# Retention plus FP4 feed-forward: in eight steps of the second half, VectorE splits the next x before it takes h's maximum instead of after h's inverse

## The reference

```
def fp4_quant_dequant(x):
    xb = x.reshape(shape[:-1] + (shape[-1] // 16, 16))
    scale = maximum(max(abs(xb), -1) / 6, 1e-12)
    xn = xb / scale
    q = GRID[searchsorted(MID, abs(xn))] * sign(xn) * scale
x1  = layernorm(x + retention(x))                # 8 heads, gate, projection
gate = fp4(x1) @ fp4(w_gate).T                   # 256 -> 704
up   = fp4(x1) @ fp4(w_up).T                     # 256 -> 704
h    = silu(gate) * up
out = layernorm(x1 + fp4(h) @ fp4(w_down).T)     # 704 -> 256
```

## Time and profile before

| | |
|---|---|
| median of 3 runs | 577.37 us |
| profiled execution | 577.54 us |
| its span in the trace | 575.6 us |
| PE busy | 558.3 us, 97% |
| DVE busy | 514.5 us, 89% |
| ACT busy | 363.9 us, 63% |
| POOL busy | 239.5 us, 42% |
| granted PE clock, mean | 0.997 |

### The profile page before, as it was taken

How to read it: one execution, slowest core, us unless ns; L and a number is a source line. 1 busy time by engine, 2 the same in 40 slices (tenths; PEclk the granted TensorE clock), 3 DMA queues, 4 the chain that set the end, 5 groups by cost and what they waited for, 6 DMA issues and landing times.

```text
span 575.6 us, 14088 instructions
## 1 busy us (share of the span) xinstructions
PE 558.3 (97%) x4408; PEld 482.1 (84%) x4408; DVE 514.5 (89%) x1193; ACT 363.9 (63%) x931; POOL 239.5 (42%) x291
## 2 busy tenths in 40 slices
PE   7999999999999999999999999999999999999993
PEld 4788888888888888888888788889999989999983
DVE  7667878999999999899999889999999999999996
ACT  4455766777686676777668654556555766676563
POOL 2211121534435344343534323665665665665430
PEclk9999999999999999999999999999999999999998
DMA  7611110110111011011001000000000110010013
GB/s 210 225 35 32 56 47 12 56 54 1 54 55 34 21 55 46 9 55 55 27 27 36 19 11 10 1 0 2 2 1 2 38 38 2 19 38 20 2 36 109
DMA packets 24984, 22.31 MB, mean 39 GB/s; under 512 B 2026, under 2 KB 21875, under 8 KB 24947
## 3 DMA queue, kind: packets, MB, share of 16 engines
q1 hardware_dynamic: 24130, 20.27, 11.4%
q10 hardware_dynamic: 816, 1.57, 0.8%
HBM read 17.63 MB, written 4.20 MB: 38 GB/s over the span
## 4 chain that ended last, share of the span: by engine, by line
PE 71%; DVE 18%; issue 5%; POOL 2%; DMA 2%; ACT 1%; DVEq 0%; ACTq 0%; POOLq 0%
PE wide_banks L1415 40%; PE wide_banks L1486 9%; PE wide_banks L1631 5%; PE wide_banks L1463 4%; DVE shared L891 3%; PE wide_banks L1474 3%; PE turn L1512 3%; PE turn L1449 2%; DVE h_amax L875 2%; DVE shared L1121 2%; PE wide_banks L1499 2%; PE wide_banks L1603 2%; DVE win_lo L1008 2%; POOL shared L1368 1%; DVE shared L896 1%
## 5 line engine op out<-in xcount | busy, mean ns | idle before, releaser
L1379 POOL TENSOR_TENSOR shared<-shared,h_scale 128x704 f32<-128x704 bf16 x31 | 43.0, 1389 | 81.9 <-DVE shared L896 79.4
L1415 PE MATMUL wide_banks<-win_hi,x_hi 128*128 128x512 f32 x192 | 65.5, 422 | 3.1 <-DVE shared L711 1.5
L1486 PEld LDWEIGHTS wide_banks<-shared 128*128 128x128 f32 x512 | 62.0, 192 | 2.8
L484 ACT ACTIVATE shared<-opened,rstd 128x64 f32<-128x64 f32 x240 | 63.5, 339 | 1.1
L1415 PE MATMUL wide_banks<-wgu_hi,xq_hi 128*128 128x512 f32 (+1 forms) x192 | 60.2, 395 | 1.4 <-DVE xq_lo L1113 1.3
L1486 PE MATMUL wide_banks<-shared 128*128 128x64 f32 x512 | 60.6, 271 | 0.0
L1415 PE MATMUL wide_banks<-win_hi,x_lo 128*128 128x512 f32 x192 | 60.3, 395 | 0.0
L1415 PE MATMUL wide_banks<-win_lo,x_hi 128*128 128x512 f32 x192 | 60.3, 395 | 0.0
L1415 PE MATMUL wide_banks<-wgu_lo,xq_hi 128*128 128x512 f32 (+1 forms) x192 | 56.5, 375 | 0.0
L1415 PE MATMUL wide_banks<-wgu_hi,xq_lo 128*128 128x512 f32 (+1 forms) x192 | 56.4, 375 | 0.0
L450 ACT ACTIVATE shared<-shared 128x704 bf16<-128x704 f32 x32 | 25.3, 789 | 44.9 <-POOL shared L1368 43.4
(11 more groups left out here) (156 smaller groups left out, 1472.3 us busy)
## 6 DMA issues: line engine op xcount, KB each, us to landing
xf<-in_x_feat SPq DMA_DIRECT2D x32, 128.0 KB, 2.2
tab<-in_tables SPq DMA_DIRECT2D x16, 256.0 KB, 2.7
xt<-in_x_tok SPq DMA_DIRECT2D x32, 128.0 KB, 2.1
out<-x SPq DMA_DIRECT2D x32, 128.0 KB, 1.7
x<-in_w_in ACTq DMA_DIRECT2D x3, 512.0 KB, 5.3
w<-in_w_gu SPq DMA_DIRECT2D x1, 1408.0 KB, 7.7
w<-in_w_down SPq DMA_DIRECT2D x1, 704.0 KB, 8.9
wgu_lo<-pow_dram SPq DMA_DIRECT2D x1, 576.0 KB, 4.8
```

What stands on the lines that cost most here:

```text
L484: last = act.activation(gated[:, b, cols], opened[:, b, cols], ACT.Copy, scale=rstd[:, b, 1 + k:2 + k])
L1379: pool.tensor_tensor(over_blocks(hq[:, b]), over_blocks(h_steps[:, b]), spread(h_fp4["scale"][:, b]), ALU.mult).then_inc(h_fp4["ready"], 1)
L1415: last = pe.matmul(dst, lhs, rhs, start=k == 0, stop=k == len(parts) - 1)
L1486: last = pe.matmul(mixed[:, r, DV * at:DV * (at + 1)], ret[:, slot(k)], vs[:, b, DV * k:DV * (k + 1)], start=False, stop=k >= HEADS - 2, s ...
```

## The change

In steps 4 to 11 (`QUAD` is 4, `EIGHT` is 8), DVE's `split_xq(n + 1)` is issued behind `add_out` and in front of `h_max(n - 1)`; in all other steps it stays behind `h_inverse`. The instruction, its operands and its semaphore wait on `xq_hi_ready` are the same. No other engine's code changes.

```diff
@@ ffn_body of DVE
                 if out:
                     add_out(n - 5, 1 - b)
+                ahead = QUAD <= n < EIGHT + QUAD
+                if ahead:
+                    split_xq(n + 1, 1 - b)
                 if quant:
                     dve.wait_ge(h_done, n)
                     h_max(n - 1)
@@
-                if valid(n + 1) and n > 0:
+                if valid(n + 1) and n > 0 and not ahead:
                     split_xq(n + 1, 1 - b)
```

## The result

The changed kernel takes 578.3 us (median of 21 runs, 577.91 to 578.57), the one before 577.37 (21 runs, 577.06 to 577.9). The ratio is 1.0015, 95% interval 1.0008 to 1.0021: slower by 0.9 us (0.5 to 1.2). I had forecast 577.2, slightly faster. The profiled execution took 578.27 us with a span of 576.2 at a granted clock of 0.997, as before.

A forecast was written before the change was run, and what follows sets the result against it. DVE's chain of waits, which releases PE at step 19, was taken to bound the kernel. Changes over steps 4 to 11 summed to -0.16 us, taken as -0.2 from the median 577.37: 577.2 us, range 576.5 to 578.3.

The forecast's parts named there:

- What bounds it: DVE's chain of waits up to PE's step 19 sets the end; PE could win back at most 2.36 us.
- Part 1: PE gets `xq_lo` about 2 us earlier, but its second part then waits for the product, so PE alone keeps no gain.
- Part 2: DVE's ordinary step, counted from `add_out`'s start: `split_h` to the product 0.21 us earlier, h's inverse 0.07 us later.
- Part 3: Which shift reaches L891: steps 6, 7 -0.21 each, 10, 11 +0.07 each, 5 0, 4 -0.07, 9 -0.09, 8 +0.28 us.
- PE keeps what it wins: Rival: PE's stalls in steps 4 to 18 are its own, up to 2.36 us back, 575.0 us; chance 0.07 of over 1.15.
- The early split waits: Rival: L1113 waits for `xq_hi` beyond step 8, or longer there; sum +0.3 to +1.0 us, 577.6 to 578.4; chance 0.12.
- The scale misses its turn: Rival: POOL's L1362 gets in before DVE's scale, reciprocal 0.59 us later; 3.1 us in all, 580.5; chance 0.13 for over 1.15.
- step 32: Evidence against the missed turn: the scale started 0.04 us ahead of L1379's recorded end and still took only 0.17 us.

The follow-up runs named there:

- the two failed mends: Changed kernel with the chain operation of steps 5 to 7 ahead of `add_out`: 579.07 us; likewise with picked split steps, early in 6, 7, 13, 14, 15: 578.64 us.

## Why the prediction was wrong

**What bounds it: right.** PE's gain of 0.74 us in step 5 was real and went to the product at once. The end moved with DVE's chain: +0.87 us from rounding to rounding over steps 4 to 18, +0.93 between the medians.

**Part 1, PE: right.** Step 5's first matmul came where PE's own queue puts it, the second part 0.05 us behind the product. I left out that from PE's step 6 on the transposes of h between the two parts can wait for `split_h`: 0.38 us of idle time in step 6 and 0.36 in step 7, marked with L1009. It didn't decide. The matmuls of the earlier trace rows at 411.29 and 418.03, which I called those of steps 10 and 11, are those of steps 11 and 12, counted from step 4 at 362.40; the 6.74 us between them stay.

**Part 2, an ordinary step of DVE: this is the step that failed.** I wrote that "the reciprocal then starts at +1.79 (was +1.72)". Steps 9, 10 and 11 did that. Steps 5, 6 and 7 have one more operation between scale and reciprocal, and my working has no term for it. It puts the reciprocal 0.03 us behind the scale's end, about as in the earlier trace rows (0.04, with the operation in between), and so takes over its 0.15 us from the trace. That duration depended on the stall I was removing: in the kernel before, the operation went in right behind a scale that had waited. It took 0.58 to 0.59 us after, and the reciprocal of these steps came at +2.19 (2.99 to 3.00 us behind the rounding, which lies at -0.81). Against the forecast that is 1.07 us over three steps. It is shown from four sides: those steps alone carry it, a short rescale of POOL removes it, an added operation with two SBUF inputs brings it to steps 9 to 11, and one with a single input doesn't.

The irony is that I had the mechanism as a rival, with the right price (0.59 later for the reciprocal), and tested it against one instruction only, the scale. The question should have been asked of every operation in the window that uses what POOL uses. There were two.

**Part 3, what reaches the next step: right.** Steps 4 and 8 to 11 came within 0.04 us each, and 5 to 7 within 0.05 once the wait was gone (+0.01, -0.26, -0.24 for 0, -0.21, -0.21).

**The rivals.** "PE keeps what it wins": out, PE's step 19 started at 466.49 instead of 465.86, later and not earlier. "The early split waits": in step 8 only, +0.24 of +0.87. "The scale misses its turn": not in this kernel, where it came 0.02 to 0.03 us ahead of POOL's start in steps 5 to 7 and 9 to 11 (0.36 in step 4) and only step 8's, held up by `xq_hi`, came inside; but it is real from 0.03 us behind that start on. What I held against it, step 32, doesn't bear on it. There the 0.17 us long scale stands directly behind another scale operation, L881, that had waited for POOL, as L1052 did in the kernel before:

```profile
555.63 0.45 DVE L881 TENSOR_SCALAR h_scale<-h_amax 128x44 f32<-128x44 f32 x1
```

The Trainium skill's rule (SBUF — State Buffer, "SBUF: two separate sides"), that the owner of the shared ports keeps them for its whole instruction, is what the traces show of DVE's side: operations that started 0.03 to 0.08 us behind a rescale of 0.62 to 0.65 us lasted 0.58 to 0.62 us, and 0.17 to 0.18 behind one of 0.24.

**The range.** It held the time (578.3, at its upper end) by luck: that end was drawn for a late `xq_hi`, and the loss came from elsewhere. The sign was wrong, and a chance of 0.80 for no measurable change says little, since +0.15% lies in it.

## What to carry to other kernels

A stall in a trace may be what lets the instruction behind it through. When an edit removes a stall at something that two engines share, don't keep the old durations of what stands behind it: list every instruction between the old and the new hand-over that contends for it, and ask for each who comes first. And count a software-pipelined loop step by step on the engine that carries the chain; the steps differ, and only their sum reaches the end.

## What the runs showed of the hardware

Who gets in is decided within 0.03 us. Taking the recorded start of POOL's rescale as zero, DVE operations that contend got through when they started at -0.03 (scale, changed kernel) or at 0.00 (the operation behind a scale that waited, kernel before), and waited for the whole instruction when they started at +0.03 to +0.05 (scale, the two failed mends) or about +0.07 (chain operation). Whether it is the start alone that decides, or also that the DVE operation ahead had been waiting, stays open: no run has a contending operation at 0.00 behind a scale that hadn't waited. POOL hardly pays when it comes second: its rescale lasts 0.64 us with such a DVE operation at its start (step 5 of the kernel before) and 0.61 to 0.62 without (steps 8 to 12).

Not every kind of operation waits there. TENSOR_SCALAR of 44 f32 columns with one SBUF input waited (0.62 us), so did TENSOR_TENSOR and SCALAR_TENSOR_TENSOR of three columns with two. RECIPROCAL of 44 and of 3 columns (0.43 and 0.17 us) and TENSOR_REDUCE (0.88 us) ran beside POOL at their usual length.

L1113 and L1008 changed length with their place: 0.36 us behind the reciprocal and 0.42 behind `add_out`, 0.81 us behind L1113 and 0.76 behind the reciprocal. Why wasn't looked into.
